# A longest-path order for four engines in a gated delta-rule attention kernel, and the second half's weights asked for by ScalarE

## The chip, the cores and the metric

One core of a Trainium2 chip. The metric is the device time of one execution, in microseconds (us). The kernel before takes 4777.71 us (median of 3 runs, 4777.23 to 4779.94).

## The reference

The input `x` is (4, 1024, 512), in float32. After a layer norm it goes through two branches: a small feed-forward branch with a router (its result `g` gates the output), and a linear attention with 8 key heads and 16 value heads of 128. All loops of this document lie in the attention.

```python
qkvz = hidden_states @ w_qkvz.T
ba = hidden_states @ w_ba.T
yc = jax.nn.silu(causal_conv_4_taps(concat(q, k, v)))
beta = jax.nn.sigmoid(b)
g = -jnp.exp(A_log) * jax.nn.softplus(a + dt_bias)
q = q * rsqrt(sum(q * q) + L2_EPS)      # k alike
def step(S, xs):
    qt, kt, vt, gt, bt = xs
    S = S * jnp.exp(gt)[..., None, None]
    kv = jnp.einsum('bhk,bhkv->bhv', kt, S)
    delta = (vt - kv) * bt[..., None]
    S = S + jnp.einsum('bhk,bhv->bhkv', kt, delta)
    o = jnp.einsum('bhk,bhkv->bhv', qt * scale, S)
    return (S, o)
xf = o * jax.nn.silu(z)
xn = xf * rsqrt(mean(xf * xf) + NORM_EPS) * norm_weight
s = xn @ w_out.T
x = x + s * jax.nn.silu(feed_forward(xn_input))
```

## The kernel before

The feed-forward branch runs first, up to about 1139 us; it writes the normalised columns of `x` to `xt_scratch` and the gate to `g_scratch`. The attention follows. It does the heads in two groups (4 key heads and 8 value heads each), since the weights of one group fill the buffer `wt`. Each group walks through all 4 sequences in **tiles** of 256 rows: 16 tiles per group, 32 in all (`TILES`). A tile has two **chunks** of 128 rows (64 in all), and a chunk two **units** of 4 value heads (128 in all).

The work per tile, the *fills*, goes through two banks of PSUM in turn: 22 `product`s (weights times the tile's columns `xtile`; 16 of them are q, k and v features, whose bank is emptied by a `lead` on ScalarE and three convolution taps on VectorE, then 2 small `ba` and 4 `z`), and transposes (`keys`, `queries`, `back`, `values`). A product has four steps k, each one matmul instruction that the trace shows as two.

The work per unit is a *build* (`scores`, `decay`), a *chain* that inverts a triangular matrix (`level` and `merge` for six levels, each with VectorE and ScalarE in between, then `error`, `first`, `second`, `third`), and a *core* with the state (`recall`, `query`, `eps`, `learn`, `answer`). Chains of two neighbouring units run side by side. Then `turn` transposes the unit's result, and once per chunk `out` multiplies with the output weights: 8 steps into one bank (`b_o`), which `dve_out` empties into `prow`. For chunks below 32 `prow` is stored as a partial result; from chunk 32 on (the second group) `dve_out` adds the partial result, and `pool_out` on GpSimd makes two passes (times gate, plus `x`) before the store.

Each engine works its queue in the order in which instructions were written; that order is made by `planned`, a list scheduler over the dependencies in `after` with durations in `TAKES` (it takes, whenever an engine comes free in its plan, one of the steps that are ready there). Which of the ready steps goes first is decided by `due`: a set position in the period of a unit or a tile. The dependencies on DMA are in no plan. SyncE's queue is written by hand: in chunk c it issues, if c is even, the load of tile c/2 + 2 into one of the two halves of `xtile`, at four chunks the weights of the second group, from chunk 32 on the loads of the rows, and last the store of chunk c, which waits for `dve_out` (below 32) or `pool_out`. TensorE's first product of a tile waits for the tile's load (semaphores `x_in0`, `x_in1`).

Of the kernel before, what the change touches and what calls it, by code (L numbers as in the profile page):

```python
# [29 lines left out]
P = 128  # L30
BATCH, T, D = 4, 1024, 512
KT = D // P
# [27 lines left out]
PERIOD = 30.0  # L60
EARLY, READY, LATE = -2.8, -1.3, 1.2
# [477 lines left out]
def planned(lanes, takes, after, due):  # L539
# [3 lines left out]
    for node, (lane, i) in place.items():  # L543
        before = [a for a in after(*node) if a in place] + ([lanes[lane][i - 1]] if i else [])
        missing[node] = len(before)
        for a in before:
            users.setdefault(a, []).append(node)
    engines = ("pe", "act", "dve", "pool")
# [8 lines left out]
    while left:  # L557
        when, engine = min((max(free[e], min(ready[a] for a in open_[e])), e) for e in engines if open_[e])
        extra = {}
        for a in open_[engine]:  # L560
            if ready[a] <= when:
                kind, cost = a[1], 0.0
                if engine == "act":
                    table = "exp" if kind in EXP else "silu" if kind in SILU else loaded
                    cost = TABLE if table != loaded else 0.0
                elif engine == "pe":
                    cost = SWITCH if narrow and kind not in SHORT else 0.0
                extra[a] = cost
        node = min(extra, key=lambda a: (due(*a) + extra[a] / PERIOD, place[a]))
        end = when + extra[node] + takes(*node)  # L570
        if engine == "act":
            loaded = "exp" if node[1] in EXP else "silu" if node[1] in SILU else loaded
        elif engine == "pe":
            narrow = node[1] in SHORT
        free[engine] = end
        open_[engine].remove(node)
        order[engine].append(node[1:])
        left -= 1
        for b in users.get(node, ()):
            lag = 0.0 if b[0] == engine else LAG[engine] + {"pe": TO_PE, "pool": TO_POOL}.get(b[0], 0.0)  # L580
            ready[b] = max(ready.get(b, 0.0), end + lag)
            missing[b] -= 1
            if not missing[b]:
                open_[b[0]].append(b)
# [9 lines left out]
def attention(nc, bank, x, cst, masks, w_qkvz, w_ba, conv_w, dt_bias, a_log, norm_weight, w_out, xt_d, g_d, part_d, out):  # L594

    with ExitStack() as ctx:
# [101 lines left out]
        def load_products(sp, g, kinds):  # L698

            for kind in kinds:  # L700
                lo, hi = W_SPANS[kind]
                if g:
                    sp.wait_ge(s["pj_ps"], (g * HALF_TILES - 1) * NP + last_prod(kind) + 1)
                    sp.wait_ge(s[f"w{kind}_in"], 16 * g)
                sp.dma_start(wt[:, :, lo:hi], w_qkvz[:, g * GROWS + lo:g * GROWS + hi].rearrange("(k p) n -> p k n", p=P)).then_inc(s[f"w{kind}_in"], 16)
# [35 lines left out]
        prod_of = {f: i for i, f in feat_of.items()}  # L741
        N_SILU = 4
# [794 lines left out]
        def after(engine, kind, *i):  # L1537
# [3 lines left out]
            if at in (("pe", "product"), ("pe", "keys"), ("pe", "queries"), ("pe", "back"), ("pe", "values")):  # L1541
# [3 lines left out]
                before = evictions(n - (f < 0), fills[f])  # L1545
                return before + {"product": [], "keys": [("act", "silu", n, 0)], "queries": [("act", "silu", n, 1)], "back": [("pool", "keys", n, i[1])],
# [39 lines left out]
            if kind == "out":  # L1586
                return {"pe": [("act", "turn", NB * n + NB - 1)], "dve": [("pe", "out", n, GV - 1)], "pool": [("dve", "out", n)]}[engine]
# [70 lines left out]
        CHAIN = {kind: k for k, kind in enumerate(["level"] + [f"{kind} {lv}" for kind, lv in [(k, lv) for lv in range(1, LEVELS) for k in ("level", "merge")]] + ["error", "first", "second", "third"])}  # L1658
        BUILD = {kind: k for k, kind in enumerate(["gate", "scores", "decay", "lower", "unit", "high", "attend", "low"])}
        CORE = {"kend": 1.8, "recall": 1.9, "query": 2.0, "eps": 2.05, "learn": 2.15, "answer": 2.2, "gated": 2.4, "norm": 2.6, "turn": 2.9}  # L1660

        def due(engine, kind, *i):

            n = i[0]
            if kind == "out":
                return NB * n + 4.0 + (0.85 * i[1] / GV if engine == "pe" else 0.9)
            if kind == "gate":
                return NB * n - 1.3
            if (engine, kind) == ("pool", "decay"):
                return n - 1.2  # L1670
            if engine == "act" and kind in ("keys", "queries", "back", "values", "lead", "silu", "ba", "z", "gates") or kind in ("product", "keys", "queries", "back", "values", "conv", "gates", "knorm", "qnorm"):
                u = UPT * n
                if engine == "pe":
                    f = fills.index((kind, *i[1:2 if kind == "product" else 3])) + (i[2] / KT if kind == "product" else 0)
                elif kind in ("lead", "conv"):
                    f = fills.index(("product", prod_of[i[1]])) + 1
                elif kind == "silu":
                    f = fills.index(("product", prod_of[(GK, 2 * GK, 2 * GK + HEADS, NF)[i[1]] - 1])) + 1.5
                elif kind in ("ba", "z"):
                    f = fills.index(("product", (2 * GK if kind == "ba" else Z0) + i[1])) + 1  # L1680
                elif kind in ("knorm", "qnorm"):
                    f = fills.index(("keys" if kind == "knorm" else "queries", CPT - 1)) + 1
                elif kind == "gates":
                    f = fills.index(("product", 2 * GK + 1)) + 2
                else:
                    f = fills.index((kind, *i[1:])) + 1
                first = fills.index(("back", CPT - 1)) + 1
                return u + (EARLY + (READY - EARLY) * f / first if f < first else READY + (LATE - READY) * (f - first) / (len(fills) - first))
            if kind in BUILD:
                return n - 1.2 + 1.1 * BUILD[kind] / len(BUILD)  # L1690
            if kind in CORE:
                return n + CORE[kind] + (0.05 if engine != "pe" else 0)
            k = CHAIN["level" if kind == "start" or kind == "level" and i[1] == 0 else f"{kind} {i[1]}" if kind in ("level", "merge") else kind]
            return n + 2.0 * (k + (0.5 if engine != "pe" else 0.0)) / len(CHAIN)

        order = planned(unit_lanes, takes, after, due)

        with nc.Block() as block:
            @block.sync
            def _(sp):  # L1700
# [5 lines left out]
                for c in range(CHUNKS):  # L1706
                    q, r = divmod(c, CPT)
                    if r == 0 and q + 2 < TILES:
                        load_tile(sp, q + 2)
                    if c == HALF_CHUNKS - 2 * CPT:  # L1710
                        load_products(sp, 1, "kq")
                    if c == HALF_CHUNKS - 2 * CPT + 1:
                        load_products(sp, 1, "vz")
# [54 lines left out]
            def _(act):  # L1768
                act_rates(act)
                for kind, *i in order["act"]:  # L1770
                    if kind == "lead":
                        act_lead(act, *i)
                    elif kind == "ba":
                        act_ba(act, *i)
                    elif kind == "z":
                        act_z(act, *i)
                    elif kind == "silu":
# [146 lines left out]
```

## Time and profile before

| | us |
|---|---|
| median of 3 runs | 4777.7 |
| the profiled execution's own time | 4782.8 |
| its span, first to last instruction | 4781.0 |
| TensorE busy in the span | 4586.8 (96%) |
| VectorE busy | 2680.7 (56%) |
| ScalarE busy | 2348.9 (49%) |
| GpSimd busy | 1387.1 (29%) |

The attention is the part from about 1139 us on. In it TensorE is busy nearly throughout, so the time is TensorE's work plus its idle time. A row of waits gives an engine, the line that waited, who released it, the total, how often, and the longest. In the rows of time the columns are start, duration, engine, line, operation and tiles; matmuls are pipelined, so the distance between two starts is the slot that the first one takes, and its duration has a tail of some 0.16 us that lies beside the next.

### The profile page before, as it was taken

To read this page: it belongs to the slowest core of one execution; us is meant where nothing else is said; L and a number is where in the kernel's file an instruction comes from. 1 tells how busy PE (TensorE), PEld (TensorE's weight loads), DVE (VectorE), ACT (ScalarE), POOL (GpSimd) and SP (SyncE) were. 2 spreads that over 40 slices of the span, in tenths; PEclk is the share of its full clock that TensorE was granted. 3 is DMA by queue.
4 is the path that set the end of the run, shared out by engine and by line. 5 is a ranking of instruction groups with operands and counts; after the bars stand their busy time and mean duration, and the time that the engine had idled before them with its cause. 6 is when DMAs were issued, how large, how long until landed. Compare 5 with 4: busy or idle time off the path is not lost.

```text
span 4781.0 us, 81715 instructions
## 1 busy us (share of the span) xinstructions
PE 4586.8 (96%) x30056; PEld 3134.5 (66%) x30056; DVE 2680.7 (56%) x6818; ACT 2348.9 (49%) x5714; POOL 1387.1 (29%) x1542
## 2 busy tenths in 40 slices
PE   7999999997899999999999999999999999999998
PEld 3444444443777777777777777777777777777775
DVE  3222222212666666666666666666676666667664
ACT  1000111101566656666666666666666666666664
POOL 1000000000233333333333333333343333434333
PEclk9999999998999999999999999999999999999998
DMA  3000000002000000000000001100000000010000
GB/s 132 19 27 25 22 24 27 18 9 94 6 10 10 10 12 10 10 10 10 10 10 17 10 28 45 34 23 23 29 26 23 23 23 23 23 37 23 23 19 30
DMA packets 72605, 118.46 MB, mean 25 GB/s; under 512 B 12432, under 2 KB 29456, under 8 KB 72208
## 3 DMA queue, kind: packets, MB, share of 16 engines
q1 hardware_dynamic: 72208, 113.22, 7.1%
q8 instruction: 242, 3.96, 0.4%
q14 instruction: 155, 1.27, 0.1%
HBM read 79.09 MB, written 34.11 MB: 24 GB/s over the span
## 4 chain that ended last, share of the span: by engine, by line
PE 63%; DVE 10%; issue 1%; ACT 1%; POOL 0%; SPq 0%; DMA 0%; DVEq 0%; POOLq 0%; ACTq 0%
PE bank L806 18%; PE bank L810 10%; PE bank L1169 9%; PE bank L1448 7%; DVE vraw L836 3%; PE bank L1086 2%; PE bank L1342 2%; PE bank L1356 2%; PE bank L1382 2%; PE bank L1294 2%; PE bank L1317 2%; PE bank L1070 1%; PE bank L945 1%; PE bank L1071 1%; PE bank L812 1%
## 5 line engine op out<-in xcount | busy, mean ns | idle before, releaser
L806 PE MATMUL bank<-xtile,wt 128*128 128x259 f32 x4096 | 1083.0, 396 | 79.2 <-DVE vraw L836 50.9
L806 PEld LDWEIGHTS bank<-xtile,wt 128*128 128x128 f32 x4096 | 725.5, 191 | 214.3 <-DVE vraw L836 81.1
L1228 ACT ACTIVATE xyinv<-bank 128x512 f16<-128x512 f32 x768 | 457.4, 596 | 365.0 <-PE bank L1169 362.5
L1206 DVE TENSOR_TENSOR wlev<-bank,mask 128x256 f16<-128x256 f32 x768 | 320.9, 420 | 469.6 <-PE bank L1169 467.0
L1448 PE MATMUL bank<-wot,xnt 128*128 128x512 f32 x1024 | 532.8, 611 | 0.9 <-ACT xnt L1441 0.8
L810 PE MATMUL bank<-wt,xtile 128*128 128x512 f32 x1024 | 523.4, 617 | 0.0
L836 DVE SCALAR_TENSOR_TENSOR vraw<-bank,taps,vraw 128x256 f32<-128x256 f32 x768 | 370.2, 482 | 126.7 <-ACT vraw L829 105.5
L370 DVE TENSOR_TENSOR hid<-bank,gate 128x512 f32<-128x512 f32 x88 | 60.9, 692 | 521.1 <-PE bank L352 521.1
L1146 POOL TENSOR_TENSOR kend<-ktok,bend 128x256 f32<-128x256 f32 x256 | 158.6, 640 | 636.3 <-issue 635.8
L1169 PEld LDWEIGHTS bank<-xyinv,lth 128*128 128x128 f16 x3584 | 220.7, 98 | 167.3 <-issue 108.5
L347 PE MATMUL bank<-h2t,wg_sb 128*128 128x512 f32 x704 | 318.4, 595 | 0.0
L352 PE MATMUL bank<-h2t,wu_sb 128*128 128x512 f32 x704 | 316.5, 592 | 0.0
L383 PE MATMUL bank<-wd_sb,hid 128*128 128x512 f32 x704 | 303.5, 592 | 0.9 <-DVE hid L370 0.9
L1121 POOL TENSOR_TENSOR ltm<-ltm,mask 128x512 f32<-128x512 f32 x128 | 148.2, 1158 | 501.5 <-DVE ltm L1104 501.5
L1169 PEld LDWEIGHTS bank<-wlev,xyinv 128*128 128x128 f16 x3072 | 187.1, 99 | 144.7 <-issue 95.0
L1169 PE MATMUL bank<-xyinv,lth 128*128 128x64 f16 (+1 forms) x3584 | 265.1, 197 | 0.9 <-ACT xyinv L1228 0.9
L829 ACT ACTIVATE vraw<-bank,taps 128x256 f32<-128x256 f32 x256 | 121.6, 475 | 282.7 <-PE bank L806 279.8
L1055 POOL TENSOR_TENSOR gm<-con,gdec 128x512 f32<-128x512 f32 x128 | 133.6, 1044 | 401.5 <-PE bank L1086 315.5
L352 PEld LDWEIGHTS bank<-h2t,wu_sb 128*128 128x128 f32 x704 | 133.8, 190 | 168.4 <-issue 168.4
L383 PEld LDWEIGHTS bank<-wd_sb,hid 128*128 128x128 f32 x704 | 133.1, 190 | 166.2 <-issue 166.2
L362 ACT ACTIVATE gate<-bank 128x512 f32<-128x512 f32 x88 | 52.6, 598 | 360.1 <-PE bank L347 360.1
L347 PEld LDWEIGHTS bank<-h2t,wg_sb 128*128 128x128 f32 x704 | 130.7, 191 | 146.0 <-issue 146.0
(179 smaller groups left out, 9327.0 us busy)
## 6 DMA issues: line engine op xcount, KB each, us to landing
xtile<-xt_scratch SPq DMA_DIRECT2D x32, 518.0 KB, 4.1
xn<-x SPq DMA_DIRECT2D x32, 256.0 KB, 5.3
xt_scratch<-xt SPq DMA_DIRECT2D x8, 1024.0 KB, 5.8
g_scratch<-sel SPq DMA_DIRECT2D x32, 256.0 KB, 2.0
wt<-w_qkvz SPq DMA_DIRECT2D x4, 2048.0 KB, 13.2
part_scratch<-prow SPq DMA_DIRECT2D x32, 256.0 KB, 2.1
prow<-part_scratch SPq DMA_DIRECT2D x32, 256.0 KB, 2.7
grow<-g_scratch SPq DMA_DIRECT2D x32, 256.0 KB, 3.5
```

Of the source, the lines that this page charges most:

```text
L347: i = pe.matmul(bank[2 + f % 2][:], wg_sb[:, k, f * P:(f + 1) * P], h2t[:, u % 2, k, :], start=(k == 0), stop=(k == KT - 1))
L352: i = pe.matmul(bank[4 + f % 2][:], wu_sb[:, k, f * P:(f + 1) * P], h2t[:, u % 2, k, :], start=(k == 0), stop=(k == KT - 1))
L383: i = pe.matmul(bank[6 + j % 2][:], hid[:, f, j * P:(j + 1) * P], wd_sb[:, f, :], start=(f == 0), stop=(f == FT - 1))
L806: j = pe.matmul(b_p[:, 0:WIN], wt[:, k, c:c + P], xtile[:, par, k, :], **st)
L810: j = pe.matmul(b_p[:], xtile[:, par, k, HALO + cc * P:HALO + (cc + 1) * P], w, **st)
L836: dve.scalar_tensor_tensor(out=acc, in0=tile_bank("product", prod_of[i])[:, tap:tap + TILE], scalar=taps[:, group(q), i, tap:tap + 1], in1 ...
L1121: pool.tensor_tensor(ltm[:], ltm[:], mask[:, M_NEG, :].unsqueeze(1).broadcast_to([P, HEADS, P]), ALU.subtract).then_inc(s["lti_sb"], 1)
L1146: i = pool.tensor_tensor(kend[:, r * REP:(r + 1) * REP], ktok[:, tile % 2, cc, m * KPB + r].unsqueeze(1).broadcast_to([P, REP, P]), bend[: ...
L1169: i = pe.matmul(dst[:, h * cols:(h + 1) * cols], lhsT(h), rhs(h), start=start and h == 0, stop=stop, skip_group_check=True)
L1206: dve.tensor_tensor(wlev[:, lv - 1].rearrange("p h (b t s) -> p h b t s", t=2, s=z)[:, :, :, 0, :], b_inv[p][:, 0:HEADS * P // 2].rearrang ...
L1228: act.activation(dst, b_inv[p][:].rearrange("p (a h b s) -> p a h b s", a=2, h=HEADS, s=z), ACT.Copy).then_inc(s[f"xy_sb{p}"], 1)
L1448: i = pe.matmul(b_o[:], xnt[:, h], wot[:, h], start=(h == 0), stop=(h == GV - 1))
```

## The change

Set due times (`PERIOD`, `EARLY`, `READY`, `LATE`, `CHAIN`, `BUILD`, `CORE` and `due`) go. In their place `planned` works out for each step the longest path that remains from it to the end, in durations and handoffs, and of the ready steps takes that with the longest (less the cost of a table load or a switch). Two dependencies are new in the plan: the first product of tile n from 2 on stands behind `dve_out` of chunk 2n-5, and `dve_out` of chunk c stands behind the last product of tile (c-1)//2. They mirror the order of SyncE's queue, without the time that it takes. The second group's weights are asked for by ScalarE, each kind right behind the last eviction of the first group's products of that kind.

```diff
-        node = min(extra, key=lambda a: (due(*a) + extra[a] / PERIOD, place[a]))
+        node = min(extra, key=lambda a: (extra[a] - path[a], place[a]))
...
+    def passes(a, b):
+        return 0.0 if a[0] == b[0] else LAG[a[0]] + {"pe": TO_PE, "pool": TO_POOL}.get(b[0], 0.0)
+
+    count, walk = dict(missing), [node for node, n in missing.items() if not n]
+    for a in walk:
+        for b in users.get(a, ()):
+            count[b] -= 1
+            if not count[b]:
+                walk.append(b)
+    path = {}
+    for a in reversed(walk):
+        path[a] = takes(*a) + max((passes(a, b) + path[b] for b in users.get(a, ())), default=0.0)
...
+        LAST_OF = {GK - 1: "k", 2 * GK - 1: "q", NF - 1: "v"}
...
+                if kind == "product" and i[1] == 0 and n >= 2:
+                    before = before + [("dve", "out", CPT * (n - 2) - 1)]
...
-                return {"pe": [("act", "turn", NB * n + NB - 1)], "dve": [("pe", "out", n, GV - 1)], "pool": [("dve", "out", n)]}[engine]
+                return {"pe": [("act", "turn", NB * n + NB - 1)], "dve": [("pe", "out", n, GV - 1), ("pe", "product", (n - 1) // CPT, NP - 1, KT - 1)], "pool": [("dve", "out", n)]}[engine]
...
-            if kind in CORE:
-                return n + CORE[kind] + (0.05 if engine != "pe" else 0)
...
-                    if r == 0 and q + 2 < TILES:
+                    if r == 0 and q < TILES - 2:
                         load_tile(sp, q + 2)
-                    if c == HALF_CHUNKS - 2 * CPT:
-                        load_products(sp, 1, "kq")
-                    if c == HALF_CHUNKS - 2 * CPT + 1:
-                        load_products(sp, 1, "vz")
...
                         act_lead(act, *i)
+                        if i[0] == HALF_TILES - 1 and i[1] in LAST_OF:
+                            load_products(act, 1, LAST_OF[i[1]])
...
                         act_z(act, *i)
+                        if i == [HALF_TILES - 1, CPT * NB - 1]:
+                            load_products(act, 1, "z")
```

**First place: TensorE at the start of a tile.** Before, the rows from the end of one tile's transposes (L945, `values`) to the next tile's first product (L806); the last `out` row ahead of them belongs to chunk 2n-4, and chunk 2n-5, behind whose store the tile's load is issued, lies a whole chunk further up.

```order
L945 MATMUL bank<-con,vraw 128x128 x4
L1169 MATMUL bank<-xyinv,lth 128x64 x4
L1294 MATMUL bank<-state,kt 128x256 x2
L1433 MATMUL bank<-con,tq 128x128 x4
L1169 MATMUL bank<-errl,errh 128x128 x4
L1169 MATMUL bank<-wlev,xyinv 128x64 x4
L1169 MATMUL bank<-xyinv,wlev 128x64 x4
L945 MATMUL bank<-con,vraw 128x128 x4
L1317 MATMUL bank<-state,qt 128x256 x2
L1169 MATMUL bank<-xyinv,lth 128x64 x4
L806 MATMUL bank<-xtile,wt 128x259
```

In the changed kernel the last step of `out` (L1459) of chunk 2n-5 itself, then learn (L1367), a level, values (L956), first (two rows of L1180), values, answer (L1393), a merge (two rows of L1180), and the first product (L817):

```order
L1459 MATMUL bank<-wot,xnt 128x512
L1367 MATMUL bank<-reps,kend 128x128 x4
L1180 MATMUL bank<-xyinv,lth 128x64 x4
L956 MATMUL bank<-con,vraw 128x128 x4
L1180 MATMUL bank<-xyinv,errh 128x128 x4
L1180 MATMUL bank<-xyinv,errl 128x128 x4
L956 MATMUL bank<-con,vraw 128x128 x4
L1393 MATMUL bank<-reps,pt 128x128 x4
L1180 MATMUL bank<-wlev,xyinv 128x64 x4
L1180 MATMUL bank<-xyinv,wlev 128x64 x4
L817 MATMUL bank<-xtile,wt 128x259 x2
```

The output of chunk 2n-5 has moved from more than half a tile's work ahead of the tile's first product to seven steps ahead of it.

**Second place: TensorE among the products of a tile.** Before, a piece a little further on, where four and more steps of `product` stand in a row (L806, a row of x7 or x8 holds two products):

```order
L1086 MATMUL bank<-gm,con 128x512
L806 MATMUL bank<-xtile,wt 128x259 x7
L1169 MATMUL bank<-wlev,xyinv 128x64 x4
L1169 MATMUL bank<-xyinv,wlev 128x64 x4
L806 MATMUL bank<-xtile,wt 128x259
```

In the changed kernel, the rows that follow on the first product of the tile:

```order
L1305 MATMUL bank<-state,kt 128x256 x2
L817 MATMUL bank<-xtile,wt 128x259 x2
L1180 MATMUL bank<-wlev,xyinv 128x64 x4
L1180 MATMUL bank<-xyinv,wlev 128x64 x4
L817 MATMUL bank<-xtile,wt 128x259
L1180 MATMUL bank<-errl,errh 128x128 x4
L817 MATMUL bank<-xtile,wt 128x259
L1328 MATMUL bank<-state,qt 128x256 x2
L817 MATMUL bank<-xtile,wt 128x259
```

The steps of a product now stand one or two at a time between steps of chain and core, so that a bank has longer to be emptied.

**Third place: TensorE at the output of a chunk.** Before, `out` (L1448) stands behind other work, while its `turn` (L1433) lies further up; in the changed kernel, for 20 of the 64 chunks in the steady part, `turn` (L1444) is directly ahead of it:

```order
L913 MATMUL bank<-con,ktok 128x128 x4
L1180 MATMUL bank<-xyinv,lth 128x64 x4
L1180 MATMUL bank<-mask,lth 128x128 x4
L1444 MATMUL bank<-con,tq 128x128 x4
L1459 MATMUL bank<-wot,xnt 128x512 x2
```

Between the two stands a copy on ScalarE (`act_turn`) that `out` waits for.

## Rows read from the trace of the kernel before

**Rows 1.** Stretches of the attention: bounds, length, busy time of each engine, granted clock.

```profile
1300.00:4700.00 3400.00, 3331.78 (x26220) 2517.26 (x26218) 2306.45 (x6006) 2127.37 (x5241) 1240.51 (x1345) 1.00 0.06 20
4700.00:4781.00 81.00, 61.60 (x462) 42.27 (x461) 30.47 (x77) 25.96 (x76) 27.49 (x30) 0.86 0.09 30
```

**Rows 2.** Waits of TensorE from 1300 to 4700 us: total, times, longest.

```profile
PE bank L806 <- DVE vraw L836: 45.3, 81, 0.8
PE bank L1169 <- ACT xyinv L1262: 10.4, 21, 0.5
PE bank L1086 <- DVE kqm L1079: 4.4, 8, 0.6
```

**Rows 3.** Groups by line from 1300 to 4700 us: busy, mean ns | idle before.

```profile
L836 DVE SCALAR_TENSOR_TENSOR vraw<-bank,taps,vraw 128x256 f32<-128x256 f32 x731 | 352.4, 482 | 111.2 <-ACT vraw L829 90.9
L1206 DVE TENSOR_TENSOR wlev<-bank,mask 128x256 f16<-128x256 f32 x737 | 308.1, 420 | 453.2 <-PE bank L1169 450.7
...
L1441 ACT ACTIVATE xnt<-bank,nw 128x512 f32<-128x512 f32 x123 | 84.8, 689 | 28.7 <-PE bank L1433 28.0
L829 ACT ACTIVATE vraw<-bank,taps 128x256 f32<-128x256 f32 x243 | 115.5, 475 | 258.4 <-PE bank L806 255.5
```

**Rows 4.** Waits of SyncE's queue.

```profile
SPq L1483 <- DVE prow L1457: 1806.2, 32, 109.0
```

**Rows 5.** Output to store to tile load, in order of time; start, duration.

```profile
2287.33 0.68 DVE L1457 COPY prow<-bank 128x512 f32<-128x512 f32 x1
2288.04 0.32 SPq L1483 DMA_DIRECT2D part_scratch<-prow  x1
2288.45 0.52 SPq L1007 DMA_DIRECT2D xtile<-xt_scratch  x1
...
3121.77 1.02 PE L1448 MATMUL bank<-wot,xnt 128*128 128x512 f32 x2
3122.83 0.69 DVE L1460 TENSOR_TENSOR prow<-bank,prow 128x512 f32<-128x512 f32 x1 [4.75 <-PE bank L1448]
...
3954.51 0.68 DVE L1460 TENSOR_TENSOR prow<-bank,prow 128x512 f32<-128x512 f32 x1
3957.92 0.34 SPq L1486 DMA_DIRECT2D out<-grow  x1
```

**Rows 6.** Issues of the group weights' loads, ns; and landing of tile loads.

```profile
L705 SPq DMA_DIRECT2D wt<-w_qkvz x8: 385/507/1347, 1155.6 to 2903.7; - x8
...
DMA to landing us min/median/max: 3.8/4.1/17.5
```

**Rows 7.** Slots of TensorE's steps, in order of time.

```profile
3015.82 0.39 PE L1169 MATMUL bank<-errl,errh 128*128 128x128 f16 x4
3016.04 0.28 PE L1169 MATMUL bank<-wlev,xyinv 128*128 128x64 f16 x4
...
3016.27 0.63 PE L945 MATMUL bank<-con,vraw 128*128 128x128 f32 x4
3016.74 1.03 PE L1317 MATMUL bank<-state,qt 128*128 128x256 f32 x4
...
3020.73 1.05 PE L1356 MATMUL bank<-reps,kend 128*128 128x128 f32 x8
3021.62 1.06 PE L1382 MATMUL bank<-reps,pt 128*128 128x128 f32 x8
...
4661.19 1.14 PE L1356 MATMUL bank<-reps,kend 128*128 128x128 f32 x8
4662.16 0.60 PE L945 MATMUL bank<-con,vraw 128*128 128x128 f32 x4
```

**Rows 8.** TensorE behind two idle times, 1195 to 1204 us.

```profile
1195.24 1.45 PE L1025 MATMUL bank<-gdec,con 128*128 128x8 f32 x6 [4.93 <-DVE gdec L999]
1196.80 3.63 PE L806 MATMUL bank<-xtile,wt 128*128 128x259 f32 x8
...
1202.56 1.80 PE L806 MATMUL bank<-xtile,wt 128*128 128x259 f32 x7 [1.69 <-DVE vraw L836]
```

More of the change, by code:

```diff
@@ L59 @@
 SCALED = 64.0
-PERIOD = 30.0
-EARLY, READY, LATE = -2.8, -1.3, 1.2
 LN_EPS = 1e-5
@@ L536, with planned @@
 SHORT = {"level", "merge", "error", "first", "second", "third"}
-def planned(lanes, takes, after, due):
+def planned(lanes, takes, after):
     place = {node: (lane, i) for lane, nodes in lanes.items() for i, node in enumerate(nodes)}
@@ L579, in planned @@
         for b in users.get(node, ()):
-            lag = 0.0 if b[0] == engine else LAG[engine] + {"pe": TO_PE, "pool": TO_POOL}.get(b[0], 0.0)
-            ready[b] = max(ready.get(b, 0.0), end + lag)
+            ready[b] = max(ready.get(b, 0.0), end + passes(node, b))
             missing[b] -= 1
@@ L696, in attention, with load_products @@
         SMALL = 16 * (3 * GROUPS + 2)
-        def load_products(sp, g, kinds):
+        def load_products(q, g, kinds):
             for kind in kinds:
@@ L702, in load_products @@
                 if g:
-                    sp.wait_ge(s["pj_ps"], (g * HALF_TILES - 1) * NP + last_prod(kind) + 1)
-                    sp.wait_ge(s[f"w{kind}_in"], 16 * g)
-                sp.dma_start(wt[:, :, lo:hi], w_qkvz[:, g * GROWS + lo:g * GROWS + hi].rearrange("(k p) n -> p k n", p=P)).then_inc(s[f"w{kind}_in"], 16)
+                    q.wait_ge(s["pj_ps"], (g * HALF_TILES - 1) * NP + last_prod(kind) + 1)
+                    q.wait_ge(s[f"w{kind}_in"], 16 * g)
+                q.dma_start(wt[:, :, lo:hi], w_qkvz[:, g * GROWS + lo:g * GROWS + hi].rearrange("(k p) n -> p k n", p=P)).then_inc(s[f"w{kind}_in"], 16)
         def load_out(sp, g):
@@ L1656, in takes @@
             return TAKES[engine, kind]
-        CHAIN = {kind: k for k, kind in enumerate(["level"] + [f"{kind} {lv}" for kind, lv in [(k, lv) for lv in range(1, LEVELS) for k in ("level", "merge")]] + ["error", "first", "second", "third"])}
-        BUILD = {kind: k for k, kind in enumerate(["gate", "scores", "decay", "lower", "unit", "high", "attend", "low"])}
-        CORE = {"kend": 1.8, "recall": 1.9, "query": 2.0, "eps": 2.05, "learn": 2.15, "answer": 2.2, "gated": 2.4, "norm": 2.6, "turn": 2.9}
@@ L1662, in due @@
[L1662 to L1690, printed above, removed]
-            if kind in CORE:
-                return n + CORE[kind] + (0.05 if engine != "pe" else 0)
-            k = CHAIN["level" if kind == "start" or kind == "level" and i[1] == 0 else f"{kind} {i[1]}" if kind in ("level", "merge") else kind]
-            return n + 2.0 * (k + (0.5 if engine != "pe" else 0.0)) / len(CHAIN)
@@ L1696, in attention @@
-        order = planned(unit_lanes, takes, after, due)
+        order = planned(unit_lanes, takes, after)
         with nc.Block() as block:
```

## The prediction

> **What bounds the kernel now.** I read the stretches first, then TensorE's waits, then what feeds it, then SyncE's queue. In the attention stage TensorE is the bound: between 1300 and 4700 us it is busy for 3331.8 of 3400 us at full clock, while VectorE has 2306 and ScalarE 2127 [rows 1]. Its work doesn't change (6880 steps in both orders), so the change can only move the 68.2 us of idle time there, the ends of the stage, and the small cost of changing between kinds of matmul. The reader is to see in the waits that 45.3 of the 68 us, in 81 pieces of at most 0.8 us, end with a convolution tap on VectorE (L836) that frees one of the two banks of the tile's products, and 10.4 and 4.4 us with `first` of the chain (L1262) and the score masks (L1079) [rows 2].
>
> **What the new order takes away.** A product's bank is free after the lead on ScalarE and three taps: 0.17 us until the last matmul's end, 0.03 + 0.48 for the lead, 3 x 0.50 for the taps with their handoffs, 0.1 for the two ends: 2.3 us [rows 3]. I laid the slots of TensorE's steps [rows 7] along both orders. Before, 88 of the 480 qkv products have less than 2.3 us of TensorE's work between their end and the next use of the bank, and lack 49 us together, against 45.3 in the trace, so the method may be trusted. After, one lacks 0.0: the products no longer stand in pairs (second pair of order pieces). `first` to `second` and `scores` to `decay` fall short of nothing either. That is **-60.1 us** (bounds: 0 and all 68.2).
>
> The switch from 16-bit to 32-bit matmuls costs 0.08 us: the same eight matmuls of L1356 take 0.97 us behind one and 0.89 behind 32-bit work [rows 7]. The orders have 1820 and 1738 such places: 82 x 0.08 = **-6.6**.
>
> **What it adds: turn and output together.** In 20 chunks `out` stands right behind `turn`, and in 7 more 0.3 us behind, while it needs ScalarE's 0.69 us copy of that turn (L1441) [rows 3]; with the matmul's tail and two handoffs 0.93 us. Nothing on TensorE can pass it, since its queue is in order: 20 x 0.93 + 7 x 0.62 = 23. Seven `turn`s stand 0.3 us behind the previous `out` and need its 0.69 us eviction: 7 x 0.65 = 5. **+28** (bounds 15 and 40: waits of ScalarE's own queue come on top or lie beside).
>
> **What it adds: the tile's input.** This decides. SyncE's queue issues the load of tile q+2 only behind the store of chunk 2q-1, and that store waits for the eviction of the chunk's output; SyncE sat 1806 us in such waits and nobody cared [rows 4], because the load was used some 66 us of TensorE's work later. The new order puts the first product of tile n behind output chunk 2n-5 by only seven steps (first pair of order pieces), the same for each n from 3 on. From the start of that chunk's last matmul pair:
> 1. to the eviction's start 1.06 us, to the store's issue 0.71, to the tile load's issue 0.41 (2.2 us in all) [rows 5];
> 2. to its landing 4.0 (median 4.1, least 3.8) [rows 6]: 6.2 us, with 0.05 to TensorE 6.25.
> 3. TensorE's work in between: the pair itself 0.86, learn 0.89, level 0.12, two transposes of values 0.94, first 0.44, answer 0.89, merge 0.23, a switch 0.08: 4.45 us [rows 7].
> So it waits 1.8 us at each of the 16 tiles 3 to 18 (chunks below 32). From chunk 32 on the store waits for GpSimd's two passes over the rows: 3.41 in place of 0.71 us from the eviction's start [rows 5]. There the wait is 4.5 us, at the 13 tiles 19 to 31. 16 x 1.8 + 13 x 4.5 = **+87**. Behind the waiting matmul is everything of TensorE, so nothing hides it; VectorE stands free at the eviction, since the step ahead of it in its order (`error`) ends 0.5 us earlier. Bounds: 1.5 and 4.2 us (landing in 3.8, shorter handoffs) give 79; 0.7 us more each (VectorE held by one tap and a half) gives 108.
>
> A wait like this also costs clock. The trace has an idle of 4.93 us, and the eight matmuls L806 behind it take 3.63 us where seven take 1.80 behind an idle of 1.69 [rows 8]: near half the speed, which is the lower of the clock's two levels, 1.2 GHz. The step lost 1.6 us, and the small one ahead of it some tenths. So I add 2.0 us to each of the 13 long waits and nothing to the short ones: **+26** (bounds 0, and twice the loss of that step, 3.2 x 13 = 42). The Trainium skill (TensorE: Matmul & The Clock Gate, "What's actually happening") says that the throttled state is the default and activity releases it; the trace agrees here, and by that rule the 16 short waits might be paid too, at 1.6 us each 26 us more; the row with 1.69 us of idle speaks against it.
>
> **ScalarE asks for the weights.** Four issues of 0.4 to 1.3 us [rows 6] leave SyncE and stand on ScalarE, which has 37% of its time free [rows 1]: 0. The z part (2 MB) goes out, in the new order, within a microsecond or two of the load of tile 16, and the two share the DMA engines: the row of the tile loads has 17.5 us as its longest, against 4.1 in the middle [rows 6]. **+4** (bounds 0 and 13, once). The Trainium skill (DMA: Bandwidth & Descriptors, "Issuing engines are not separate DMA queues") says the same: another issuing engine saves only the time to issue. By it the move gains nothing, and by the longest row it would cost 13 in place of 4.
>
> **Ends and tightness.** In the last 81 us TensorE idles 19.4 [rows 1], mostly for the last units' chains; the new order starts unit 127's chain with 39 us of TensorE's work still left ahead of the last output, not 27, so more of it is covered: **-8** (-15 to 0). The first two tiles go out in a thicker burst against the same taps: **+3** (0 to 8). The inversion chain stands tighter: from a level's matmuls to their merge 1.6 us of work in the middle, before 2.7, where 0.7 is the least (VectorE's 0.42 [rows 3] and handoffs); 112 places are within 0.5 us of that, before 30. **+8** (0 to 33).
>
> Sum: -60.1 - 6.6 + 28 + 87 + 26 + 4 - 8 + 3 + 8 = +81. The profiled execution took 4782.8 us (span 4781.0 and 1.8 around it), which is 5.1 us above the median of 4777.7; I add to the median: **4859 us**.
>
> **Rivals.**
> - *The input arrives in time* (faster). If stalls between output and product, or a quicker landing, cover the load, the terms of 87, 26 and 4 fall away: 4778 - 36 = 4742. For it speaks that the waits of L806 go for certain. Against it: 4.45 us of work against 6.25, and 8.95 in the second half. It decides from 36 / 29 = 1.2 us of wait per tile downwards; I have 1.8 and 4.5.
> - *Only the short wait* (a little slower). If GpSimd's leg is hidden, all 29 tiles wait 1.8 and the clock stays: 52 in place of 113, so 4859 - 61 = 4798. Nothing supports it: the two passes are on the way to the store in the trace [rows 5], and the change leaves them.
> - *The chain is too tight* (slower still). If VectorE has something else in front at half of the 112 tight places and each pays 1 us, 56 more: 4915. Against it: 30 places were as tight before, and no wait that they could cause is among the three largest [rows 2].
> - *Balance.* The waits for the input just make good the 60 us: no mechanism, chance alone.
>
> **Chances.** Forecast 0.70 (its own range 4810 to 4900: low bounds of wait, clock and tightness; high bounds of one or two of them), input in time 0.10, only the short wait 0.08, too tight 0.10, balance 0.02. Faster by over 0.2% (9.6 us, about what a measurement of this kernel can tell) 0.11, within it 0.03, slower 0.86. The range takes in the short wait and leaves out the fast rival and the far end: 4790 to 4905.
>
> **What would show it.** TensorE's waits have a new first row: the first product matmul of a tile behind the DMA of `xtile`, 29 times, in two groups near 1.8 and 4.5 us; the waits on L836's successor shrink under 10 us in the middle stretch; half-clock stretches appear once per tile after about 3000 us, none in the steady part before; `out` shows waits on ScalarE's turn copy of some 20 us; and a tile takes some 4.7 us longer in the second half than in the first (2.7 of wait, 2.0 of clock). I am wrong if that first row is missing or under 35 us in total, or if the granted clock never falls after the long waits.

## Result, and the profile after

The changed kernel takes 4888.3 us (median of 4 runs, 4882.9 to 4891.0), the kernel before on the same chip 4777.5: 1.0229 times as long, interval 1.0212 to 1.0247. The forecast of 4859 was on the right side with the right first cause, and 29 us too low.

The stretches of the attention and its last 81 us in the changed kernel, as in [rows 1] (TensorE alone: bounds, length, busy time, granted clock, share and rate of the DMA engines):

```profile
1139.00:1300.00 161.00, 122.06 (x735) 0.88 0.21 69
1300.00:4808.00 3508.00, 3352.93 (x26182) 0.98 0.06 19
4808.00:4889.20 81.20, 67.13 (x483) 0.95 0.13 43
```

In the middle TensorE is now idle for 155.1 us, before for 68.2 [rows 1], and the clock, which was at its full 2.4 GHz throughout, is not any more. Its waits from 1300 to 4800 us, as in [rows 2]:

```profile
PE bank L817 <- DMA xtile<-xt_scratch: 96.5, 29, 5.8
PE bank L1180 <- DVE wlev L1217: 30.8, 19, 3.9
PE bank L1459 <- ACT xnt L1452: 15.9, 21, 0.8
PE bank L817 <- DVE vraw L847: 4.5, 8, 0.6
PE bank L1444 <- DVE prow L1468: 2.6, 4, 0.6
PE bank L1444 <- DVE prow L1471: 1.9, 3, 0.6
```

The 45.3 us behind the taps are 4.5, the second and third row of before are gone, and in their place stands a new first row: 29 tiles wait for their input. One of the long ones, in order of time (start, duration, engine and line, in brackets the idle before):

```profile
3468.29 0.69 DVE L1471 TENSOR_TENSOR prow<-bank,prow 128x512 f32<-128x512 f32 x1 [0.45 <-PE bank L1459]
3469.06 1.28 POOL L1478 TENSOR_TENSOR grow<-prow,grow 128x512 f32<-128x512 f32 x1 [7.63 <-DVE prow L1471]
...
3470.42 1.27 POOL L1480 TENSOR_TENSOR grow<-grow,xrow 128x512 f32<-128x512 f32 x1
...
3471.72 0.34 SPq L1497 DMA_DIRECT2D out<-grow  x1
...
3472.16 0.53 SPq L1018 DMA_DIRECT2D xtile<-xt_scratch  x1
...
3476.17 2.10 PE L817 MATMUL bank<-xtile,wt 128*128 128x259 f32 x4 [4.42 <-DMA xtile<-xt_scratch]
```

This is the path that the prediction drew: VectorE's eviction, GpSimd's two passes (the 3.43 us from the eviction's start to the store's issue are the 3.41 of [rows 5]), store, tile load, 4.0 us to the landing, product. At full clock the four matmuls of L817 take 1.14 us; here 2.10.

### The profile page after: what moved, and what is told of

Read it like the earlier page. It is cut to its first block, busy times and chain, and to the rows that moved or that the text cites. A ratio compares the mean times of both kernels' runs of the same rounds, so it can differ in the third digit from the quotient of the medians.

```text
span 4889.2 us, 81671 instructions
## 1 busy us (share of the span) xinstructions
PE 4615.8 (94%) x30056; PEld 3147.7 (64%) x30056; DVE 2697.4 (55%) x6818; ACT 2298.0 (47%) x5669; POOL 1384.9 (28%) x1542
## 4 chain that ended last, share of the span: by engine, by line
PE 64%; DVE 5%; DMA 3%; issue 1%; POOL 1%; ACT 0%; SPq 0%; DVEq 0%; POOLq 0%; ACTq 0%
PE bank L817 18%; PE bank L1180 9%; PE bank L821 9%; PE bank L1459 9%; DMA xtile<-xt_scratch 3%; PE bank L1353 2%; PE bank L1305 2%; PE bank L1097 2%; PE bank L1367 2%; PE bank L1328 2%; PE bank L1393 2%; PE bank L1081 1%; PE bank L823 1%; PE bank L1082 1%; PE bank L1444 1%
## 5 line engine op out<-in xcount | busy, mean ns | idle before, releaser
L817 PE MATMUL bank<-xtile,wt 128*128 128x259 f32 x4096 | 1129.0, 403 | 133.6 <-DMA xtile<-xt_scratch 96.5
L817 PEld LDWEIGHTS bank<-xtile,wt 128*128 128x128 f32 x4096 | 735.3, 195 | 250.2 <-DMA xtile<-xt_scratch 100.6
L1459 PE MATMUL bank<-wot,xnt 128*128 128x512 f32 x1024 | 541.8, 623 | 16.7 <-ACT xnt L1452 16.7
L821 PE MATMUL bank<-wt,xtile 128*128 128x512 f32 x1024 | 533.5, 616 | 0.0
L1180 PEld LDWEIGHTS bank<-wlev,xyinv 128*128 128x128 f16 x3072 | 185.3, 98 | 252.2 <-issue 143.5
L1180 PEld LDWEIGHTS bank<-xyinv,lth 128*128 128x128 f16 x3584 | 221.3, 99 | 137.4 <-issue 94.1
L1180 PE MATMUL bank<-xyinv,lth 128*128 128x64 f16 (+1 forms) x3584 | 263.1, 198 | 2.0 <-ACT xyinv L1239 1.5
L1180 PE MATMUL bank<-wlev,xyinv 128*128 128x64 f16 x3072 | 214.4, 193 | 31.8 <-DVE wlev L1217 31.2
L847 DVE SCALAR_TENSOR_TENSOR qt<-bank,taps,qt 128x256 f32<-128x256 f32 x384 | 185.1, 482 | 88.0 <-ACT qt L840 80.7
L360 ACT ACTIVATE gate<-bank 128x512 f32<-128x512 f32 x88 | 52.6, 597 | 360.0 <-PE bank L345 360.0
```

The costliest lines, as they stand in the source:

```text
L817: j = pe.matmul(b_p[:, 0:WIN], wt[:, k, c:c + P], xtile[:, par, k, :], **st)
L821: j = pe.matmul(b_p[:], xtile[:, par, k, HALO + cc * P:HALO + (cc + 1) * P], w, **st)
L847: dve.scalar_tensor_tensor(out=acc, in0=tile_bank("product", prod_of[i])[:, tap:tap + TILE], scalar=taps[:, group(q), i, tap:tap + 1], in1 ...
L1180: i = pe.matmul(dst[:, h * cols:(h + 1) * cols], lhsT(h), rhs(h), start=start and h == 0, stop=stop, skip_group_check=True)
L1459: i = pe.matmul(b_o[:], xnt[:, h], wot[:, h], start=(h == 0), stop=(h == GV - 1))
```

## Experiments

"x wait" is the total of TensorE's waits for `xtile`; a half-clock stretch is one in which the records grant 1.2 GHz, counted from 1380 to 4660 us, so between the start and the end, which have some in every kernel; the changed kernel has 27 there (the texts written beforehand say 29 and 21, counted over other stretches), the kernel before none. Busy and idle times of TensorE are from 1139 us on, where the attention's products begin. The kernel before took 4778 to 4782 us beside these runs. They were made on three chips: the early load, the load ahead of the store and the two runs on who asks for the weights on one; the second run of the changed kernel, the first dose of idle-time matmuls, the eased rule and the gates on another; the second dose, the third run of the changed kernel, the turn's copy and the last run on a third.

**The tile's load two chunks earlier.** Only SyncE's queue changes:

```diff
-                    if r == 0 and q < TILES - 2:
-                        load_tile(sp, q + 2)
+                    if c == 0:
+                        load_tile(sp, 2)
+                    if r == 0 and q < TILES - 3:
+                        load_tile(sp, q + 3)
```

> The changed kernel, with the same order on all four computing engines. SyncE's queue alone differs: it issues the load of each tile from the third on behind the store of chunk 2n-7 in place of 2n-5, two chunks earlier. My theory (the new order lost on the late input and on the clock that it costs): the 96.5 us of waits for xtile in the stretch 1300 to 4800 fall under 5 us, the half-clock stretches of the steady part fall from 29 to under 5 (they cost some 40 us), the waits on wlev (30.8 us) and on turn and output (20 us) stay, and the time falls from 4888 by 96 + 40 to about 4750 (4735 to 4775), below the kernel before. Rival A (the order is slower in itself: the chain too tight, more waits behind VectorE): the x waits go and others come in their place, 4790 to 4830. Rival B (the clock has nothing to do with the waits): 4888 - 96 = 4792, with as many half-clock stretches as now.

Measured: 4741.5 us, 0.992 of before (0.9907 to 0.9932). TensorE's steps stand in the same order as in the changed kernel, record by record, so the late load is the whole of the loss: the new order in itself is faster than the old, by 0.8%. Its waits from 1300 to 4800 us:

```profile
PE bank L1180 <- DVE wlev L1217: 30.5, 19, 3.9
PE bank L1459 <- ACT xnt L1452: 16.7, 22, 0.8
PE bank L1444 <- POOL tq L1435: 5.1, 1, 5.1
PE bank L817 <- DVE vraw L847: 4.2, 7, 0.6
```

No row of `xtile` is left, the others stand as they were, and of the half-clock stretches 4 remain. (The row of 5.1 us belongs to the program's end, which has moved into this window.) Rivals A and B both fall.

**The tile's load ahead of the odd chunk's store.** It waits for VectorE's eviction, not for GpSimd and not for the store's issue:

```diff
+                    if r == 1 and q < TILES - 3:
+                        sp.wait_ge(s["po_sb"], c + 1)
+                        load_tile(sp, q + 3)
                     store(sp, c)
```

> The changed kernel, with SyncE issuing the tile's load ahead of the odd chunk's store in place of behind it: it waits for VectorE's eviction of that chunk's output, but not for GpSimd's two passes over it and not for the store's own issue. My theory says that GpSimd's leg is what makes the second half's waits long: all 29 waits become one size, 1.2 to 1.6 us (now 1.6 to 2.5 in tiles 3 to 18, 4.4 to 5.8 in tiles 19 to 31), 35 to 48 us together in place of 96.5; the clock falls in fewer places, and the time is 50 to 85 us below the changed kernel: 4803 to 4838. Rival (the long waits come from the DMA engines being busier in the second half, not from the queue): the second half's waits stay above 3.5 us, and the time falls by 15 to 25 us only.

Measured: 4794.2 us, 1.0032 (1.002 to 1.0044). The x wait is 43.9 us in 28 pieces, the half-clock stretches 7. A wait of the first and one of the second half:

```profile
2538.81 1.15 PE L817 MATMUL bank<-xtile,wt 128*128 128x259 f32 x4 [1.42 <-DMA xtile<-xt_scratch]
...
3438.36 1.14 PE L817 MATMUL bank<-xtile,wt 128*128 128x259 f32 x4 [1.09 <-DMA xtile<-xt_scratch]
```

The 4.4 us of the second half are now 1.0 to 1.2 at eight of its twelve tiles: GpSimd's leg made them long, and not a slower transfer. The time is 9 us below the 4803 to 4838 expected. The changed kernel was not run on this chip; against its runs on others (4876.0 to 4888.3) the gain is 82 to 94 us, where 50 to 85 were expected, and 47.6 to 52.6 of them are x wait.

**Weights asked for by ScalarE, in the order of before.** The issues move as in the change; nothing else does (the same two lines behind `act_z`, and `LAST_OF`, are left out here):

```diff
-                    if c == HALF_CHUNKS - 2 * CPT:
-                        load_products(sp, 1, "kq")
-                    if c == HALF_CHUNKS - 2 * CPT + 1:
-                        load_products(sp, 1, "vz")
...
+                        if i[0] == HALF_TILES - 1 and i[1] in LAST_OF:
+                            load_products(act, 1, LAST_OF[i[1]])
```

> The kernel before with its own order; only the second group's weights are asked for by ScalarE, as in the changed kernel. My theory: this half of the change is worth nothing by itself, 0 (-3 to +3 us), since SyncE's queue was free to issue them and ScalarE has time. Rival: ScalarE's queue blocks on the waits that stand ahead of the issues (the last product of each kind of the tile), and the leads behind them come late: +3 to +15 us, with a wait of TensorE on ScalarE near 2200 us.

Measured: 4781.6 us, 0.9999 (0.999 to 1.0008). This half of the change is worth nothing by itself.

**Weights asked for by SyncE again, in the new order.** All four parts behind the load of tile 16, and none by ScalarE:

```diff
+                    if c == HALF_CHUNKS - 2 * CPT:
+                        load_products(sp, 1, "kqvz")
...
-                            load_products(act, 1, LAST_OF[i[1]])
...
-                            load_products(act, 1, "z")
```

> The changed kernel with its order, but the second group's weights asked for by SyncE again, all four parts in a row behind the load of tile 16. My theory: in this order SyncE reaches that place only just ahead of tile 16's first product, so the weights come late: that product waits 8 to 20 us once (now 5.7), and the time is 3 to 15 us above the changed kernel, 4891 to 4903. The other 28 waits for xtile stay as they are. Rival (ScalarE's issues cost more than SyncE's, through leads that come late): the time is the same or up to 10 us lower.

Measured: 4875.2 us, 1.0201 (1.0185 to 1.0216), which looked like a gain. The changed kernel itself was therefore run once more:

> The changed kernel as it is, once more, on the same chip as the three kernels beside it, so that they can be compared. My theory: 4882 to 4892 us again, 96 us (90 to 100) of waits for xtile. Rival, since the run with the weights on SyncE came out 13 us below the changed kernel: its waits differ from chip to chip by the landing time of the load, and this run may be 4870 to 4880.

Measured: 4876.0 us, 1.0195 (1.018 to 1.0211). My expectation of 4882 to 4892 was wrong, and the rival's 4870 to 4880 came true, with 91.5 us of x wait in place of 96.5. So no difference by who asks for the weights can be told in the new order either (the two runs are from different chips), and my theory of late weights was wrong: tile 16's product waited 4.4 us, with ScalarE asking 5.65. The 12 us belong to the runs of the changed kernel: 4888.3, 4876.0, and later 4882.8.

**TensorE kept at work while it waits.** Before the wait for `xtile` stand matmuls without a reader, into the bank that the product then fills. The first dose was 5 and 14:

```diff
+                if i == 0 and q >= 3:
+                    bank_for(pe, q, "product", i)
+                    for _ in range(5 if q < 19 else 14):
+                        pe.matmul(tile_bank("product", i)[:, 0:WIN], xtile[:, 1 - par, 0, 0:P], xtile[:, 1 - par, 0, :], start=True, stop=True)
```

> The changed kernel; while TensorE waits for the tile's input it now does matmuls whose result nobody reads, into the bank that the first product then fills anew: 5 of 128x259 (1.4 us at full clock) at tiles 3 to 18, 14 (4.0 us) at tiles 19 to 31. The input lands when it did, so only what the idle time did to the clock is taken away. My theory (the clock costs 40 to 50 of the 147 us between this kernel and the one with the early load): the half-clock stretches of the steady part fall from 29 to under 5, and the time is 35 to 50 us below the changed kernel, 4838 to 4855. Rival (the clock's fall is unrelated to the idle time, or its cost lies in the waits already): no change, or 5 to 10 us above it.

Measured: 4870.1 us, 1.0186 (1.0171 to 1.0201), 6 us below the run beside it. The dose was wrong, as one row shows (14 matmuls have 28 records):

```profile
3465.88 6.36 PE L811 MATMUL bank<-xtile 128*128 128x259 f32 x28
```

They took 6.4 us where 4.4 were idle, so the product started late. The run said nothing on the price of the clock. With smaller numbers, and the changed kernel beside it:

```diff
-                    for _ in range(5 if q < 19 else 14):
+                    for _ in range(3 if q < 19 else 8):
```

> The first run with idle-time matmuls gave them too much: one takes 0.445 us, not 0.28, so 14 took 6.3 us where 4.4 were idle, and 5 took 2.2 where 1.8 were. Here 8 at tiles 19 to 31 (3.6 us) and 3 at tiles 3 to 18 (1.3 us), all within the wait for the tile's input; otherwise the changed kernel as before. My theory (the clock costs 36 to 45 of the 135 us between the changed kernel and the early load on this chip): half-clock stretches in the steady part from 21 to under 8, the input's landing and so the start of the first product where it was, and the time 30 to 42 us below the changed kernel beside it (4834 to 4846 if that is 4876). Rival (the first overdose hid nothing, the clock is worth under 15 us): 4861 or more.

> The changed kernel as it is, as the partner of the run with idle-time matmuls on this chip: 4870 to 4890.

Measured: 4849.1 us, 1.0151 (1.0137 to 1.0165), against 4882.8, 1.0222 (1.0206 to 1.0238). One wait, of the same tile in both; first the changed kernel, then the one with the matmuls (its L821 is L817):

```profile
3465.29 2.10 PE L817 MATMUL bank<-xtile,wt 128*128 128x259 f32 x4 [4.46 <-DMA xtile<-xt_scratch]
```

```profile
3454.48 3.74 PE L811 MATMUL bank<-xtile 128*128 128x259 f32 x16
3459.07 1.14 PE L821 MATMUL bank<-xtile,wt 128*128 128x259 f32 x4 [0.85 <-DMA xtile<-xt_scratch]
```

The engine stands just as long between the last useful step and the product (3.6 + 0.85), yet the product runs at full speed. The time falls by 33.7 us, within the 30 to 42 expected. In the two profiled executions the half-clock stretches fall from 22 to 7 and the span by 26.6 us: 1.8 us for each, or 2.2 by the medians.

**The planner's own rule eased.** On top of the early load, the dependency of a tile's first product moves from chunk 2n-5 to 2n-7:

```diff
-                    before = before + [("dve", "out", CPT * (n - 2) - 1)]
+                    before = before + [("dve", "out", CPT * (n - 3) - 1)]
```

> The kernel with the early load, and the planner's own rule for it eased to match: the first product of tile n may stand behind output chunk 2n-7 in place of 2n-5, so its order changes. My theory: the 31 us of waits on wlev and 17 + 5 us on turn and output come of what VectorE and ScalarE have in front of them and not of this rule, so the time stays within 8 us of 4741. Rival (the rule pushes the products together and the chain aside): 10 to 25 us faster, with the wlev waits under 15 us.

Measured: 4740.8 us, 0.9914 (0.9899 to 0.9928), with the same waits to 0.4 us, though part of the order changes. The rule costs nothing.

**The gates at their measured length.** On top of the early load:

```diff
-                return 3.2 if i[1] else 0.7
+                return 4.2 if i[1] else 0.9
```

> The kernel with the early load; the planner is told that VectorE's gates take 4.2 us and 0.9 in place of 3.2 and 0.7, and orders by that. My theory: the waits on wlev (30.5 us in 19 pieces, VectorE being in the gates, which take 3.9 to 4.4 us while GpSimd works beside it) come of that number: they fall under 12 us, and the time by 10 to 25 us, to 4717 to 4732. Rival (the wait only moves: VectorE's long block stands in front of something in any order): waits on VectorE as a whole stay at 35 to 45 us, and the time within 6 us of 4741.

Measured: 4726.6 us, 0.9885 (0.9868 to 0.9901). First its waits from 1300 to 4800 us:

```profile
PE bank L1459 <- ACT xnt L1452: 22.1, 29, 0.8
PE bank L1180 <- DVE wlev L1217: 10.5, 14, 2.2
```

Two thirds of the waits on `wlev` came of a duration that was too short, and the time fell by 14 to 15 us. The gates block (L998 to L1010) takes 3.87 or 3.88 us at 25 of the 32 tiles of the changed kernel, where the planner counted 3.2; at three in its second half it takes 4.5. What adds the last 0.7 us is seen at one of these, ahead of a wait of 3.13 us (the largest is 3.9):

```profile
3533.26 1.45 POOL L1478 TENSOR_TENSOR grow<-prow,grow 128x512 f32<-128x512 f32 x1
...
3533.51 1.23 DVE L1055 TENSOR_SCALAR ngam<-gex 128x8 f32<-128x8 f32 x1
...
3535.29 0.84 DVE L1000 TENSOR_SCALAR ratio<-yneg 128x16 f32<-128x16 f32 x1
...
3539.39 0.42 DVE L1217 TENSOR_TENSOR wlev<-bank,mask 128x256 f16<-128x256 f32 x1
...
3539.87 0.39 PE L1180 MATMUL bank<-wlev,xyinv 128*128 128x64 f16 x4 [3.13 <-DVE wlev L1217]
```

**The turn's copy told longer.** On top of the gates, ScalarE's copy between `turn` and `out` is planned longer:

```diff
-("act", "turn"): 0.70
+("act", "turn"): 1.40
```

> The kernel with the early load and the longer gates (4726.6); the planner is further told that ScalarE's copy of the turn takes 1.40 us in place of 0.70, so that it does not count on the output right behind the turn. TensorE's slots laid along the new order leave 8 chunks with the output straight behind the turn, before 27. My theory: the 22 us of waits of output on ScalarE's copy fall to 6 to 9, the others stay, and the time falls by 12 to 20 us to 4707 to 4715. Rival (the steps that now stand between turn and output only bring the same wait to another place, or the longer path through the output delays the tile's products): waits of 10 us or more in new rows, time within 6 us of 4727.

Measured: 4702.6 us, 0.9842 (0.9829 to 0.9856), the fastest: 75.5 us below before. The fall of 24 us is more than the 12 to 20 expected. From 1300 to 4700 us it waits:

```profile
PE bank L817 <- DVE vraw L847: 9.5, 28, 0.6
PE bank L1180 <- DVE wlev L1217: 7.0, 8, 3.0
PE bank L1459 <- ACT xnt L1452: 6.2, 8, 0.8
```

Waits of `out` are 6.2 us in 8 places, as laid out beforehand, and of half-clock stretches one is left. By the profiled spans 15 of the 29 us are idle time and 14 busy time.

**More allowance everywhere.** On top of the gates, more for that copy, and a longer lag behind every step of VectorE:

```diff
-LAG = {"pe": 0.25, "act": 0.06, "dve": 0.06, "pool": 0.06}
+LAG = {"pe": 0.25, "act": 0.06, "dve": 0.3, "pool": 0.06}
...
-("act", "turn"): 0.70
+("act", "turn"): 1.80
```

> As the kernel beside it, with 1.80 us told for ScalarE's copy of the turn and 0.30 us in place of 0.06 for what lies between VectorE's end and the next engine's start (what the trace shows there is nearer to 0.1 to 0.2, and VectorE is often late by a tap). My theory: turn and output wait 1 us together, and the places where a level's merge stands tight behind VectorE are half as many, so the waits on wlev stay under 8 us: 4700 to 4712, the fastest of all. Rival (the planner's order gets looser where TensorE needs its products: more idle at the tile's banks): 4715 to 4735.

Measured: 4774.6 us, 0.9992 (0.9983 to 1.0). My expectation was wrong by 65 us and the rival right, and too mild. From 1300 to 4700 us:

```profile
PE bank L817 <- DVE vraw L847: 32.0, 25, 2.5
PE bank L1180 <- DVE wlev L1217: 17.6, 17, 2.5
PE bank L1180 <- ACT xyinv L1239: 8.3, 12, 0.7
```

`out` waits 0.2 us, as meant, but VectorE now has its score masks in front of the taps of a product:

```profile
2138.04 1.60 DVE L1115 SCALAR_TENSOR_TENSOR ltm<-gam,beta,kqm 128x128 f32<-128x128 f32 x4
...
2139.57 1.51 DVE L847 SCALAR_TENSOR_TENSOR vraw<-bank,taps,vraw 128x256 f32<-128x256 f32 x3
...
2141.14 1.29 PE L817 MATMUL bank<-xtile,wt 128*128 128x259 f32 x3 [2.48 <-DVE vraw L847]
```

Against the kernel with the turn's copy at 1.40 TensorE is idle 32 us more and busy 44 us more. Of the 44, slots under half clock (14 more stretches) are 35 when each record's slot is set against its usual length at full clock; 5 are the ends of matmuls that stand alone before a wait, and 4 are spread over the other slots. Eight of its 15 stretches stand at no wait longer than 1.6 us, but at three short ones close together:

```profile
3357.84 0.29 PE L1180 MATMUL bank<-wlev,xyinv 128*128 128x64 f16 x4 [0.61 <-DVE wlev L1217]
...
3358.93 0.29 PE L1180 MATMUL bank<-xyinv,lth 128*128 128x64 f16 x4 [0.69 <-ACT xyinv L1239]
3360.79 1.23 PE L817 MATMUL bank<-xtile,wt 128*128 128x259 f32 x2 [1.57 <-DVE vraw L847]
```

From 3360.1 us, within the third of these waits, to 3366.9 the granted clock is 0.50. Two numbers were changed in this run at once, so it doesn't say which of them did the harm.

## Why the prediction was right, and where its sizes were not

Span against span the change costs 108.2 us (4889.2 less 4781.0): 77.9 of idle and 30.3 of busy time. Term by term, predicted and measured:

| term | predicted | measured | from |
|---|---|---|---|
| waits taken away | -60.1 | -55.6 | [rows 2] 60.1 less the 4.5 left |
| waits for the input, with the collision | +87 +4 | +96.5 | first row of the waits |
| turn and output | +28 | +20.4 | 15.9 + 2.6 + 1.9 |
| chain tighter | +8 | +28.0 | 30.8, before 2.8 |
| other small waits | none | -2.4 | what is left of the middle's 86.9 |
| start, end | +3, -8 | -3.7, -5.3 | idle 42.6 to 38.9, 19.4 to 14.1 |
| clock | +26 | +49.6 | busy 3542.1, with the early load 3492.5 |
| rest of the busy time | -6.6 | -19.3 | 30.3 less 49.6 |

The terms miss in both directions: the clock and the chain came out 44 us above the forecast, the turn, the start and the rest of the busy time 27 us below, and part of the nearness of 4859 to 4888 is that luck.

**The input.** Right in mechanism, place and size: 1.7 to 2.5 us at tiles 3 to 18, but for tile 16, and 4.4 to 4.9 at most of the later ones, for 1.8 and 4.5 forecast. Tiles 22, 26 and 30 waited 5.6 to 5.8, which I had not seen. There GpSimd has just begun another step when the eviction ends, and its two passes start a microsecond later, as at tile 22:

```profile
3587.86 0.68 DVE L1471 TENSOR_TENSOR prow<-bank,prow 128x512 f32<-128x512 f32 x1
3588.53 1.19 POOL L1157 TENSOR_TENSOR kend<-ktok,bend 128x256 f32<-128x256 f32 x2 [6.52 <-issue]
3589.67 1.28 POOL L1478 TENSOR_TENSOR grow<-prow,grow 128x512 f32<-128x512 f32 x1
```

Tile 31 waited 2.7. At tile 16 the load landed 7.9 us after its issue in place of some 4, and the wait was 5.65 us, 3.2 and 3.7 more than at its neighbours, for 4 forecast. The early load takes all of it away, the load ahead of the store takes GpSimd's leg away, and each does what the path says.

**The clock** is the term that was sized too small. The price per long wait was near: by the granted clock in the 8 us behind each, TensorE lost 34 us behind the 14 long waits (tile 16 and tiles 19 to 31), 2.4 each for 2.0 forecast. Per half-clock stretch the comparisons give 1.8 to 2.6 us: against the early load, in busy time, 49.6 us for 23 stretches, 35.8 for 14 in the second run of the changed kernel and 40.4 for 18 in the third, and 1.8 with the idle-time matmuls. The count was wrong. The step "none for the short waits" failed: I took it from the one row with 1.69 us of idle [rows 8]. Here are three rows of the changed kernel:

```profile
1651.99 1.87 PE L817 MATMUL bank<-xtile,wt 128*128 128x259 f32 x4 [2.12 <-DMA xtile<-xt_scratch]
...
2553.75 1.14 PE L817 MATMUL bank<-xtile,wt 128*128 128x259 f32 x4 [2.02 <-DMA xtile<-xt_scratch]
...
2664.59 1.15 PE L817 MATMUL bank<-xtile,wt 128*128 128x259 f32 x4 [2.10 <-DMA xtile<-xt_scratch]
```

The first is in a half-clock stretch. The second is followed by none. The third looks alike, but the clock falls behind its four matmuls, as the stretch that begins 1.4 us after their start shows:

```profile
2666.00:2669.40 3.40, 3.40 (x11) 0.50 0.00 0
```

So ten of its 15 short waits were followed by a half-clock stretch, eight of them before 3000 us, where "What would show it" had none; they cost 17 us, 1.7 each. In its second run, with waits of 1.46 to 2.08, two of 15 were, and in its third five. That is also most of why its runs differ: between the profiled executions of the first and the second, 15 of the 21 us are slots under half clock. A short wait is paid for in some places and runs and not in others. The sentence in the prediction that gave the 16 short waits 26 us more, by the Trainium skill (TensorE: Matmul & The Clock Gate, "What's actually happening"), was nearer to this run than the row I set against it. Four more stretches stand behind waits on `wlev` of 3.1 to 3.9 us, which the clock term left out altogether; the early load has four such stretches too, so they are not in the 49.6.

**The chain** was the second mis-sized term, and by its step: I counted places within 0.5 us of the least distance and gave them 8 us. The distance was not the trouble. At all 19 places VectorE was in the gates block, and `wlev`, whose turn comes after it, was late by up to 3.9 us. The tightness rival asked for just this, VectorE with something else in front, but at half of 112 places with 1 us each.

**The rest of the busy time.** The traces of before and after settle it when each record's slot (the distance to the next start) is set against the usual slot of its kind at full clock. Slots under half clock are 51 us more, near the 49.6 above. The end of a matmul, some 0.16 us that otherwise lies under the next one, stands alone before 131 idle times where it did before 196: 10 us less. The slots at full clock are 10 us less, for the 6.6 that 82 fewer switches were to give. The prediction had no term for the ends.

**Rivals.** "Input in time" is the kernel with the early load: its price of 4742 against 4741.5 measured. That is luck in part: some 20 us too little for `wlev` and 13 too much busy time, with smaller terms, offset each other in it. "Only the short wait" is what the load ahead of the store comes to (4798 forecast, 4794.2 measured), and in the changed kernel nothing hid GpSimd's leg. ScalarE's issues are 0, as said.

## What to carry to other kernels

When a schedule is made denser, look at each transfer whose issue stands in a queue behind the work that was moved: a load that nobody waited for becomes the first wait if its issue keeps its place in the program and its use does not. Then price the idle time twice, once for itself and once for the clock behind it. And a planner that places by the longest path is only as good as its durations: two numbers set a little above what the trace shows (gates) or well above it (the turn's copy) brought 39 us, while an allowance on every step of VectorE, with still more for that copy, cost 72.

## What the hardware showed that I had not expected

- The clock falls behind idle times of about 2 us, but not each time: in the changed kernel 1.81 us brought a half-clock stretch, 2.02 did not; in the kernel with the load ahead of the store 1.91 was followed by 2.07 us for the four matmuls, 1.95 and 2.20 by 1.15. It also falls where waits of 0.61, 0.69 and 1.57 us stand close together, as in the last run. The Trainium skill (TensorE: Matmul & The Clock Gate, "Why this matters for your kernels") warns of longer idle times only; by these rows that is too generous in work that is otherwise dense.
- The clock can fall a microsecond and more behind the end of the wait (1.4 us at 2664.59), so the length of the first matmuls behind a wait doesn't tell whether it was paid for; the granted clock does.
- Matmuls that nobody reads keep the clock up through a wait, and are worth 33.7 us here.
- A small step of VectorE can last as long as the GpSimd pass beside it: L1055 on 128x8 took 1.23 us until 3534.74, where GpSimd's pass ended at 3534.71, and 0.16 us elsewhere (3066.51). It was slow 15 times of 64, each time beside such a pass. L1000 took 0.84, to the end of the next pass, and elsewhere 0.17. Not every step is held: L998, which started 0.02 us behind that same pass, took its usual 0.16. The Trainium skill (SBUF — State Buffer, "SBUF: two separate sides") calls the pair of ports between the two an exclusive lock; for L1055 and L1000 the trace agrees.
